# GpSimd splits the encoder weights in pieces of 512 columns instead of 256

## What is computed

```python
h = _L0_tok_ref(x, ...)                       # patches -> tokens, plus a class token
h = h + _L0_attn_ref(_layernorm(h), ...)      # causal attention with rotary positions
h = h + _L0_ffn_ref(_layernorm(h), ...)       # 16 experts, top-74 tokens each, and a shared one
h = h + _L1_attn_ref(_layernorm(h), ...)      # an encoder of 6 layers, below
h = h + _L1_ffn_ref(_layernorm(h), ...)       # gated FFN with weights and inputs rounded to fp4
```

```python
q, k, v = x @ Wqkv.T + bqkv
x = _ln(x + attention(q, k, v) @ Wo.T + bo, ln1_g, ln1_b)
x = _ln(x + gelu(x @ W1.T + b1) @ W2.T + b2, ln2_g, ln2_b)   # W1: 1024x256, W2: 256x1024
```

## Time and profile before

| what | value |
|---|---|
| median of three runs | 831.51 us |
| profiled execution | 829.94 us, its span 828.1 us |
| DVE busy | 635.5 us, 77% |
| ACT (ScalarE) busy | 461.2 us, 56% |
| POOL (GpSimd) busy | 266.9 us, 32% |
| granted TensorE clock, mean | 0.994 of full speed |
| L1993 W_L, 128x256 | 96 instructions, 70.8 us, mean 777 ns |
| L1993 WQKV_L, 128x256 | 36 instructions, 25.7 us, mean 750 ns |

### The profile page before, as it was taken

The page is one execution under the profiler, slowest core; times in us unless marked ns, Lnnn a source line. Parts: engine busy times, 40 slices in busy tenths (PEclk is TensorE's granted clock), DMA queues, the critical chain, the costliest instruction groups (busy, mean ns, idle before and its releaser), DMA issues.

```text
span 828.1 us, 16419 instructions
## 1 busy us (share of the span) xinstructions
PE 798.5 (96%) x5958; PEld 745.2 (90%) x5958; DVE 635.5 (77%) x1277; ACT 461.2 (56%) x829; POOL 266.9 (32%) x307
## 2 busy tenths in 40 slices
PE   5999999999999999999999999999999999999987
PEld 4998789999999999899989989998998999999667
DVE  5687594787788776778797887878778797875596
ACT  3277424333333336585776777677687766745421
POOL 0002130411111100364365146336525623633243
PEclk9899999999999999999999999999999999999999
DMA  5001746988889812010310021021011102010001
GB/s 188 1 1 52 316 149 235 332 312 313 318 318 331 329 61 106 2 39 14 102 40 0 18 96 38 13 101 38 9 44 61 38 13 101 24 82 1 1 1 30
DMA packets 18290, 88.36 MB, mean 107 GB/s; under 512 B 3120, under 2 KB 7472, under 8 KB 12240
## 3 DMA queue, kind: packets, MB, share of 16 engines
q1 hardware_dynamic: 18256, 87.90, 30.2%
HBM read 85.05 MB, written 2.84 MB: 106 GB/s over the span
## 4 chain that ended last, share of the span: by engine, by line
PE 48%; issue 22%; POOL 17%; DVE 10%; ACT 2%; DMA 0%; POOLq 0%; DVEq 0%; SPq 0%; ACTq 0%
PE bank L1134 14%; PE bank L1171 6%; POOL W_L L1993 5%; POOL HF_L L2047 4%; POOL arena L1974 4%; POOL WQKV_L L1993 3%; PE bank L888 2%; DVE OB L2166 2%; PE bank L1180 2%; PE bank L744 2%; PE bank L1044 2%; PE bank L786 2%; PE bank L721 2%; PE bank L903 2%; PE bank L801 2%
## 5 line engine op out<-in xcount | busy, mean ns | idle before, releaser
L1134 PE MATMUL bank<-arena 128*128 (+1 forms) x1024 | 117.8, 274 | 0.0
L1134 PEld LDWEIGHTS bank<-arena 128*128 128x128 f32 x1024 | 117.4, 192 | 0.0
L1974 POOL TENSOR_TENSOR arena<-arena,srec 111x456 f32<-111x456 f32 x56 | 52.4, 963 | 129.4 <-DVE srec L2154 129.4
L1993 POOL TENSOR_TENSOR W_L<-LW,W_H 128x256 fp32r<-128x256 f32 x96 | 70.8, 777 | 29.2 <-DVE XHL L2590 25.8
L2047 POOL TENSOR_TENSOR HF_L<-arena,HF_H 128x296 fp32r<-128x296 f32 x48 | 43.8, 935 | 86.5 <-ACT HF_H L1889 86.5
L786 PE MATMUL bank<-XHL,W_H 128*128 128x296 f32 x288 | 66.4, 308 | 1.2 <-DVE arena L2143 1.2
L1889 ACT ACTIVATE arena<-bank,vec 128x296 f32<-128x296 f32 x96 | 48.9, 509 | 24.6 <-PE bank L786 17.8
L2005 POOL TENSOR_TENSOR QW<-QW,arena x14 | 22.4, 1601 | 119.0 <-DVE QW L2491 65.6
L1325 PE MATMUL bank<-HF_L,W_H 128*128 128x296 f32 x192 | 57.4, 299 | 0.0
L1325 PE MATMUL bank<-HF_H,W_H 128*128 128x296 f32 x192 | 57.4, 299 | 0.0
L1325 PE MATMUL bank<-HF_H,W_L 128*128 128x296 f32 x192 | 57.3, 299 | 0.0
(11 more groups left out here) (274 smaller groups left out, 2224.4 us busy)
## 6 DMA issues: line engine op xcount, KB each, us to landing
arena<-ew_in SPq DMA_DIRECT2D x16, 2048.0 KB, 8.9
arena<-ew_in SPq DMA_DIRECT2D x16, 1024.0 KB, 6.7
LW<-lw_in SPq DMA_DIRECT2D x12, 1024.0 KB, 4.9
arena<-route SPq DMA_DIRECT2D x32, 185.0 KB, 3.4
LW<-lw_in SPq DMA_DIRECT2D x6, 768.0 KB, 4.4
fp_weights<-arena SPq DMA_DIRECT2D x1, 2048.0 KB, 6.4
arena<-fp_weights SPq DMA_DIRECT2D x1, 2048.0 KB, 7.2
arena<-patches_in SPq DMA_DIRECT2D x2, 864.0 KB, 7.8
```

Of the source, the lines that this page charges most:

```text
L1134: last = mm(o[:, m * CAP:(m + 1) * CAP], w[:, kc, mi * P:(mi + 1) * P], xg(kc, e), start=(kc == 0), stop=(kc == C - 1))
L1974: nc.gpsimd.tensor_tensor(v, v, srec[0:QROWS, s:s + 2, :].unsqueeze(3).to_broadcast([QROWS, 2, C * JH, KEYS]), ALU.mult).then_inc(p_ready, 1)
L1993: last = nc.gpsimd.tensor_tensor(low[:, cols], value[:, cols], high[:, cols], ALU.subtract)
```

## The change

The constant that `split_part` steps by is doubled, so each of its instructions takes 512 columns.

```diff
@@ -48,7 +48,7 @@
 FI = 704
 FC = 6
-LOW_COLS = 256
+LOW_COLS = 512
 FTAIL = FI - (FC - 1) * P
```

## The result

The changed kernel takes 834.21 us (median of 20 runs, 830.97 to 837.55) against 829.25 for the kernel before (median of 20 runs on the same chip, 825.75 to 834.7). The ratio is 1.0065, its 95% interval 1.0050 to 1.0081, so about 5.4 us slower with an interval of 4.1 to 6.7 (the two medians differ by 4.96). I had predicted 835.4, range 830 to 840, by +3.9 us.

What follows compares the result with a forecast made beforehand. TensorE, busy 96% of the span, was taken as the bound, so only what makes PE wait counts. Terms 3.8 + 0.3 - 0.2 = +3.9 us on 831.5 gave 835.4 us, range 830 to 840.

Steps and rivals of the forecast that it cites:

- The length of a piece: GpSimd's 512-column piece: 1.27 us long, starts 1.23 apart, from a line through 256 and 1280 columns; bounds 1.16 and 1.35.
- rival B: GpSimd's piece is much longer, from 1.38 us, and the kernel slower by over 1%; chance 0.07.
- Term 1: Input stream's low part: second L2590 waits for a longer piece, PE with it; 0.64 us in six first phases, +3.8 us.
- Term 2: RSUM ends earlier, but the copy behind it later, delaying variance and scale; 0.07 us five times, +0.3 us.
- Term 3: Wqkv's low part is ready earlier, so PE's first product with it gains 0.04 us a layer, -0.2 us in all.
- A: DVE does not wait for a whole GpSimd piece, as the port goes over at an inner step; 831 us, chance 0.12.
- C: Pieces 1.09 us apart or less put the first L2590 under the fifth piece; +5.5 us, 837, chance 0.16.
- D: PE does not wait longer, since something behind makes up for DVE's delay; 831 us, chance 0.05.
- The comparison between the two phases: L2590 ends 0.94 us later in the first phase and PE takes 0.93 longer, so DVE's delay reaches PE in full.

Runs made afterwards that it cites:

- Experiment 3: The changed kernel, but GpSimd starts W2's pieces only when DVE's L2590 of the same phase is done; ratio 0.9946 to the kernel before.
- experiment 8: The changed kernel with W1 and W2 in pieces of 1024 columns and no added waits; ratio 1.0165 to the kernel before.
- experiment 2: The change for Wqkv alone, in pieces of 512, with W1 and W2 left at 256; ratio 1.0000 to the kernel before.
- experiment 4: The changed kernel with W1 and W2 in pieces of 128, Wqkv in 512, no added waits; ratio 1.0287 to the kernel before.
- experiment 7: The changed kernel with W1 and W2 in pieces of 128, held back behind DVE's L2590 and vector copy; ratio 1.0000 to the kernel before.

## Why the prediction was right, point by point

**The length of a piece.** 1.27 us forecast; undisturbed ones take 1.26 us, and three for Wqkv take 3.72, so they start 1.23 apart, as forecast. The line through 256 and 1280 columns holds; the bounds of 1.16 and 1.35 were not needed. The upper one was worked out too low: from 0.727 to 0.829 us over 40 columns is 2.55 ns a column, which gives 1.38 us, the very point at which rival B begins.

**Term 1.** +0.64 us a first phase forecast; the six steps of PE between the first L801 and the scores are 0.69, 0.68, 0.66, 0.66, 0.67 and 0.67, in all 4.03 against 3.8. The second L2590 ends at 505.49, 2.01 us behind the start of L801, where it ended 1.36 behind. Experiment 3 takes the wait away and the loss goes, experiment 8 doubles the piece and the loss comes out as worked out by the same steps. One row of the changed kernel shows that not every DVE instruction is held:

```profile
L2698 DVE SCALAR_TENSOR_TENSOR XD<-CN,lvec,bank x48: 503/515/523, 357.6 to 778.2; 128x296 f32<-128x296 f32 x48
```

XD has L2590's width and reads one tensor from SBUF and one from PSUM; 22 of its 48 begin while a piece of L1993 runs, 11 of them lie wholly within one, and none takes over 523 ns.

**Term 2.** PE's mean product 0.11 us earlier, its variance 0.20 later against that: +0.08 us five times, 0.4 us, against 0.07 and 0.3. The copy took 1.25 us as forecast, RSUM 0.82 against 0.77.

**Term 3.** The 0.04 itself was read from no row. The first product does come 0.046 to 0.048 earlier, and it does not last; experiment 2 gives +0.02 for the whole encoder instead of -0.2. This term was mis-sized: I had counted an earlier start of one product as time saved, though the second product, 0.3 us on, stands where it stood.

**The sum.** 3.9 against 4.39 in the encoder; of the 0.5 between them 0.2 is term 1, 0.2 term 3 and 0.1 term 2. The timed 5.4 has 4.39 within its interval. The +6.8 of the two profiled spans must not be read as the change: 1.40 of it is a stretch at half clock. That 835.4 lies only 1.2 us from the measured 834.21 is in part luck: the 831.51 that I started from was 2.3 above the median of 20 runs, and the change was put 1.1 to 1.5 too low. From 829.25 the same +3.9 gives 833.1.

**Rivals.** A (no whole-piece wait) falls with experiment 8. B (a longer piece) and C (another phase) did not occur: L2590 fell under the fourth piece in all six. D (no wait of PE) falls with the 0.66. The comparison between the two phases, on which the passing on of DVE's lateness rested, overstated the port's share of what was already lost (0.93 against 0.71), but the added delay did pass on in full.

**What I had not seen.** Shorter is not simply better. By my steps pieces of 128 were to be 4 us faster and were 23.8 slower, since I had read the handing over at the end of a piece from rows with instructions of 256 columns and more.

## What to carry to other kernels

A GpSimd instruction's length is a latency for a DVE instruction beside it that reads two SBUF tensors, and a piece size set by GpSimd's own overhead can cost a critical DVE instruction more than it saves. Find in the trace the DVE instructions whose duration differs between places and whose end lies a fixed step behind a GpSimd end, and move GpSimd's work behind them with a wait that already has its semaphore (here -0.55%) before tuning its size. If it can't be moved, don't cut it very short: back-to-back pieces of 0.46 us kept DVE out until the last one, and 192 columns (0.6 us) was the best of the sizes tried without the waits.

## What the hardware showed

- A DVE instruction that is held (296 columns, two SBUF inputs) ends 0.32 to 0.33 us behind GpSimd's instruction, for GpSimd instructions of 0.5 to 2.4 us. XD, with one input in SBUF and one in PSUM, is not held. A 14-column copy from SBUF to SBUF ends 0.03 behind and is held as well: 1.26 us instead of 0.17.
- The port was handed over at the end of the running piece in every case seen at 192 columns and above. At 128 the first L2590 waited for all the pieces left (13 of them) in seven of twelve first phases, and at 160 (10 of them) in one of six. In three of the other five at 128 it waited for the running piece and one more (0.89 to 0.90 us), in two at most for the running one (0.53 and 0.64). Which phases it hits differs between two executions of one program. The Trainium skill, page "SBUF — State Buffer", section "Who interferes with whom", says that whichever issues first has the shared pair for its whole instruction and the other fully blocks. By that rule each wait would end with the running piece; the trace agrees from 192 columns up, and not always at 160 and 128, where the measurement decides. I did not find what decides it: the next piece starts 0.11 to 0.14 us behind DVE's start in most cases of both kinds, and 0.28 behind it in one case of each. That the gap-free following of the next piece is the reason is only argued, not shown; pieces of 128 with a gap between them weren't tried.
- Stretches at half the granted clock stand at varying places, also where PE had hardly idled: the one at 750 us came in three of the thirteen executions. In the changed kernel's, PE is recorded busy for all but 0.12 of the 7.5 us before it, 1.4 of them with products one column wide, and it cost 1.40 us. Around the end of PE's waits of 4.7 us in experiment 4 there was one each time.
- The waiting goes both ways: beside DVE's L2707 in pairs, two GpSimd pieces of 128 columns lasted 1.48 and 1.33 us instead of 0.46 (experiment 7).
